# Regrouping the probability blocks on their way back from DRAM: one transfer per 32 destination partitions, or one per quarter of every partition's row

## The reference

```python
q = (query @ wq).reshape(bs, sq, HQ, DK).transpose(0, 2, 1, 3)
k = (key @ wk).reshape(bs, sk, HKV, DK)
v = (value @ wv).reshape(bs, sk, HKV, DV)
...
scores = jnp.einsum('bhqd,bhkd->bhqk', q, k) / scale
attn = jax.nn.softmax(scores + m[:, None, :, :], axis=-1)
out = jnp.einsum('bhqk,bhkd->bhqd', attn, v)
out = out.transpose(0, 2, 1, 3).reshape(bs, sq, HQ * DV)
return out @ wo
```

## Time and profile before

| | us |
|---|---|
| median of 3 runs | 1771.52 (1771.15 to 1772.29) |
| the profiled execution | 1774.46 |
| its span, first to last instruction | 1772.7 |
| TensorE busy | 1736.4 |
| VectorE busy | 1101.1 |
| GpSimd busy | 782.3 |
| ScalarE busy | 733.5 |

### The profile page before, as it was taken

One profiled execution on the slowest core, in us unless ns is written; L12 is line 12 of the kernel. 1 busy time (PEld: TensorE's weight loads), 2 busy tenths in 40 slices (PEclk: granted clock), 3 DMA queues, 4 the chain that ended last, 5 costly groups with the idle time before them and its releaser, 6 DMA issues.

```text
span 1772.7 us, 26431 instructions
## 1 busy us (share of the span) xinstructions
PE 1736.4 (98%) x8904; PEld 1579.1 (89%) x8904; DVE 1101.1 (62%) x2116; ACT 733.5 (41%) x1532; POOL 782.3 (44%) x588
## 2 busy tenths in 40 slices
PE   6999999999999999999999999999999999999998
PEld 6999999999888888888999999889999899999986
DVE  7631276566433333336666668898888888888845
ACT  5211210012333232222101014477887888888724
POOL 3223522125422222201222234487787877877634
PEclk9999999999999999999999999999999999999999
DMA  4212442235643333423433335699999999999833
GB/s 140 63 49 83 133 133 84 85 104 162 208 128 119 111 116 118 128 82 95 129 109 91 106 113 163 200 291 272 274 277 274 270 275 281 276 272 281 257 117 111
DMA packets 186403, 291.55 MB, mean 164 GB/s; under 512 B 48337, under 2 KB 146897, under 8 KB 185281
## 3 DMA queue, kind: packets, MB, share of 16 engines
q1 hardware_dynamic: 186304, 290.33, 55.7%
HBM read 193.01 MB, written 97.26 MB: 164 GB/s over the span
## 4 chain that ended last, share of the span: by engine, by line
PE 70%; DMA 8%; DVE 5%; POOL 2%; issue 2%; ACT 2%; SPq 1%; DVEq 0%; ACTq 0%; POOLq 0%
PE bank L200 65%; DMA probabilities<-q_rotated_then_x_rows 3%; DMA e_raw_wo<-in_wo 3%; SPq L1761 1%; DVE e_scores L1696 1%; POOL shared_operand_low L324 1%; PE bank L106 1%; DVE q_rotated_then_x_rows L1739 1%; PE bank L2317 1%; DVE e_p_t_low L1982 1%; PE bank L186 1%; PE bank L2330 1%; DMA aw_weights_then_ctx_rows<-in_wv 1%; DMA aw_weights_then_ctx_rows<-in_wk 0%; DMA ctx_raw<-in_ctx_t 0%
## 5 line engine op out<-in xcount | busy, mean ns | idle before, releaser
L200 PE MATMUL bank<-shared_operand_high,w_first_high 128*128 128x448 f32 (+1 forms) x768 | 279.1, 363 | 1.9 <-DVE shared_operand_low L558 1.2
L200 PE MATMUL bank<-shared_operand_high,w_first_low 128*128 128x448 f32 (+1 forms) x768 | 278.4, 362 | 0.0
L200 PE MATMUL bank<-shared_operand_low,w_first_high 128*128 128x448 f32 (+1 forms) x768 | 278.3, 362 | 0.0
L324 POOL TENSOR_TENSOR shared_operand_low<-ctx_raw,shared_operand_high 128x768 fp32r<-128x768 f32 x64 | 119.2, 1875 | 199.6 <-ACT shared_operand_high L320 199.4
L1704 ACT ACTIVATE e_scores<-e_scores,e_least 128x375 f32<-128x375 f32 x256 | 153.5, 601 | 44.9 <-DVE e_least L1696 44.9
L1452 POOL TENSOR_TENSOR w_first_low<-aw_weights_then_ctx_rows,w_first_high 128x1024 fp32r<-128x1024 f32 x30 | 72.2, 2407 | 221.1 <-ACT w_first_high L1420 221.1
L200 PEld LDWEIGHTS bank<-shared_operand_high,w_first_high 128*128 128x128 f32 x768 | 144.7, 188 | 13.1 <-POOL w_first_low L496 1.4
L200 PEld LDWEIGHTS bank<-shared_operand_low,w_first_high 128*128 128x128 f32 x768 | 144.8, 189 | 11.0
L200 PEld LDWEIGHTS bank<-shared_operand_high,w_first_low 128*128 128x128 f32 x768 | 144.6, 188 | 11.0
L320 ACT ACTIVATE shared_operand_high<-ctx_raw 128x768 fp32r<-128x768 f32 x64 | 52.8, 843 | 211.8 <-DMA ctx_raw<-in_ctx_t 193.2
L1696 DVE CUSTOM_DVE_ANT_0 e_scores<-bank,e_mask_then_layer_ffn 128x375 f32<-128x375 f32 x256 | 134.8, 529 | 0.0
(11 more groups left out here) (259 smaller groups left out, 4614.7 us busy)
## 6 DMA issues: line engine op xcount, KB each, us to landing
probabilities<-q_rotated_then_x_rows SPq DMA_DIRECT2D x64, 768.0 KB, 4.7
ctx_raw<-in_ctx_t SPq DMA_DIRECT2D x64, 384.0 KB, 3.9
e_shuffled_then_xn_t<-probabilities SPq DMA_DIRECT2D x128, 192.0 KB, 3.9
e_shuffled<-probabilities SPq DMA_DIRECT2D x128, 192.0 KB, 3.9
e_raw_wo<-in_wo SPq DMA_DIRECT2D x64, 256.0 KB, 4.8
aw_weights_then_ctx_rows<-in_wq SPq DMA_DIRECT2D x30, 512.0 KB, 4.0
q_rotated<-q_rotated_then_x_rows SPq DMA_DIRECT2D x64, 224.0 KB, 2.3
e_raw_then_a<-q_rotated SPq DMA_DIRECT2D x64, 224.0 KB, 5.0
```

Of the source, the lines that this page charges most:

```text
L200: mm = pe.matmul(out, stationary[a], moving[b], start=(first and i == 0), stop=(last and i == 2))
L324: pool.tensor_tensor(k.ctx_ring[1][slot][:, 2 * j:2 * j + 2, :], k.c_raw[:, j % 2], f32(k.ctx_ring[0][slot][:, 2 * j:2 * j + 2, :]), ALU.s ...
```

## The change

The same 768 KB move from `probabilities` to `pt_raw`, still in four transfers of 192 KB, in pieces of 384 values (1536 bytes) on both sides. They are grouped the other way round. Before, transfer j filled the 32 partitions of key block j with all four query blocks: the destination is 32 partitions by 4 by 384, the source is walked as (a: 32 rows, i: 4, 384). After, transfer i fills column block i of all 128 partitions: the destination is 128 partitions by 384, the source is walked as (j: 4, a: 32, 384). The waits, the semaphore and its count of 64, and the place in SyncE's order are the same.

```diff
-        for j in range(BLOCKS):
-            sp.dma_start(self.pt_raw[t][BLOCK * j:BLOCK * (j + 1)],
-                         self.k.p_dram[t, :, j].rearrange("(i a) x -> a i x", i=BLOCKS)).then_inc(
-                self.shuffled[t], 16)
+        for i in range(BLOCKS):
+            sp.dma_start(self.pt_raw[t][:, i], self.k.p_dram[t, BLOCK * i:BLOCK * (i + 1)].rearrange(
+                "a j x -> j a x")).then_inc(self.shuffled[t], 16)
```

## The result

The changed kernel takes 2143.54 us (median of 4 runs, 2137.36 to 2144.99) where the kernel before takes 1771.9 us beside it. The ratio is 1.2088, with a 95% interval of 1.2061 to 1.2114. The prediction was 2136, its range 1975 to 2400.

What follows compares the result with a forecast made beforehand. TensorE was taken to set the pace, DMA engines following with almost no slack. 357 us over 61 steps, plus 12, less 5, gave +364 on 1774.5: 2138.5, or 2136 as median; range 1975 to 2400.

Steps and rivals of the forecast that it cites:

- The mechanism: Block reads in attention steps: source outermost count 4 puts each transfer on the same 4 of 16 DMA engines; forecast 0.74.
- The first effect: Block transfers back: 128 partitions instead of 32 could go at 423 GB/s instead of 231, 1.5 us less DMA work per step.
- The step: One attention step on a loaded engine: 9.6 + 3.9 + 1.3 = 14.8 us instead of 8.95, bounds 12.6 and 18.8.
- The blocks' term: Blocks on a loaded engine, each step: 196,600 bytes at the middle rate of 20.4 GB/s, 9.6 us.
- the other bytes and the gap: Rest of a loaded engine's step: 104,200 bytes at 26.4 GB/s, 3.9 us, plus 1.3 us unfilled before blocks are read.
- the lower bound of 7.4: Least time in us for a loaded engine's blocks in a step, at 26.4 GB/s taken from the write out's 423.
- The estimate of 6.8 us: Blocks' share of a step at the page's about 27 GiB/s for an engine, somewhat below the prediction's lower bound.
- Rival 3: Block reads: four engines also stand in each other's way, staying at 14.4 GB/s; 2370 us; chance 0.13.
- The intervals: 61 step intervals, `carry_out` of step 2 to that of step 63, each 5.85 us longer: 357 us.
- 12 us on steps 0 and 1: Blocks of steps 0 and 1, in the queries' stage with weight tiles queued behind: 6 us added on each.
- 5 us of slack: Head start from blocks issued two steps ahead: 4 to 5 us, spent once in the first step, subtracted from the total.
- The granted clock: TensorE in the attention steps: cost of a lower clock from idling put at nothing; at 1.2 GHz its part would be 17.5 us.

Runs made afterwards that it cites:

- the two kernels with wide sources: Changed kernel with narrow writes regrouping: reads kept as four transfers with 128 source rows outermost, 1789.19 us; or one wide read, 1792.39 us.
- the kernel with two engines: Changed kernel with each quarter transfer cut into two of 64 partitions, source outermost count 2: 2621.89 us, ratio 1.482 against the kernel before.

## Why the prediction was right, point by point

**The mechanism.** Four engines instead of sixteen: shown, by the five updates of each transfer's semaphore where there were sixteen, and by the runs: going back to sixteen with the same destinations takes 354 of the 372 us away, and halving and doubling the bytes on a loaded engine moves the step with them. That the transfers share the same four is shown by the write's landings: twelve parts early, four late. Which of the sixteen they are, no run shows. By the Trainium skill ("DMA: Bandwidth & Descriptors", "Why a DMA increments its semaphore by 16 and not by 1") the count is the largest number up to 16 that divides both outermost counts; the runs with outermost counts of 128, 4 and 2 on the DRAM side, with 16, 4 and 2 engines by their semaphores, agree.

**The first effect,** wider destinations being faster, was real: 305 and 326 GB/s for wide reads in the two kernels with wide sources, against 230 for narrow ones. It is less than the 423 that I had taken from the write out: in the write's window there are no packets of the size of keys and values, which I had put "in the mix" of it "or behind it"; they come behind it. It has packets of 6144 bytes, and of 2048 from a `wo` tile. In the change the first effect is buried. On its own it was never isolated, since each kernel that had it paid for it with narrow writes.

**The step: 14.8 forecast, 14.64 measured.** The blocks' term was 9.6 us, the other bytes and the gap 3.9 + 1.3 = 5.2 us. From the first block packet to the last it is 10.25, and the rest is 4.5. So each part was within 16%, one too low and one too high, and the two errors cancel (the two measured parts are of steps 6 to 61, 14.76 us on average). The blocks' term was right by luck: the middle of two rates was a choice for want of a row, and neither end was the pace. Alone the four engines need 8.0 us, more than the lower bound of 7.4, which came from packets of 6144 bytes; what brings the time up to 10.25 is the slow start and the slower pace while all sixteen engines are busy, and neither was in the prediction. The estimate of 6.8 us was too low as well. Rival 3 had the four in each other's way at 14.4 GB/s for an engine; 196,600 bytes in 10.25 us are 19.2. The rest is shorter because the gap is: queries, keys and V keep the four busy until 1.0 us after the block issue, and the first block packet starts 0.3 us later, where I had 1.3. The sentence that the four engines go from one step's work to the next without another gap was right, and so was the place of `carry_out`, which is issued at least 7.1 us before it is needed.

**The intervals** were 61 times 14.64 - 8.95 = 5.69 us, 347 us, where 357 was forecast. The profiled spans differ by 2141.5 - 1772.7 = 368.8, where the sum had 364. `carry_out` of step 2 comes 5.1 us later (1140.58 against 1135.48), where I had put 12 us on steps 0 and 1. What follows `carry_out` of step 63 grew from 91.5 to 107.6 us (to the ends of the two spans), where I had written that it is unchanged and taken 5 us of slack off the whole. That term failed: the last write lands 5.8 us later after its issue (10.6 us to the blocks' issue, where it was 4.8), the `wo` behind the last blocks comes late as well, and nothing covers them at the end. 10 us too many in the steps, 7 too many at the start and 21 too few at the end: that the total is within 5 us is luck again.

**The granted clock.** I put it at nothing, on the ground that idling had not lowered it. That ground was wrong: the clock of the stage fell from 1.00 to 0.84. It still cost the steps nothing, for a reason that I had not given: in each of them the write out waits at least 7.1 us in the queue of the four engines. In the step shown TensorE ends its work at 1531.0 us and waits for the blocks until 1533.7. After `carry_out` of step 63 nothing covers it, the clock there is 0.88 (0.98 before) and TensorE is busy for 86.9 us instead of 81.6; up to 5 of the 16 us can be the clock's, which no run isolates.

**The signs.** 167 GB/s (165 said), TensorE's share 0.71 (0.6, as I left the lower clock out), its waits at the split of the blocks, landings of the blocks 4.8 to 10.5 us after their issues (5 to 12): as said. The DMA share of 0.54 lies above the 0.4 to 0.5 that I gave.

## What to carry to other kernels

When a transfer is regrouped, look at the outermost count on both sides, not only at the number of partitions and the piece: here a 4 on the DRAM side undid 128 partitions on the other and cost 21%, with bytes, pieces and issue count unchanged. A mean DMA share of 0.54 can hide engines that are full: look for a floor at k/16 in the slices (0.25 here for four engines), and for transfers of unchanged shape that all land late. A chain of waits that passes through a landing does not show that the landing is needed so early: count the time by which the next transfer is issued before its engines come to it, 7.1 us or more here. And where a load stands in a queue behind a long wait, another engine's queue can be worth more than a faster transfer: 7.5 to 10 us on the kernel before, for a few lines.

## What the runs showed of the hardware that I had not expected

TensorE's clock falls within a step and comes back. Windows of the changed kernel: a stretch in which TensorE issues nothing (1515.0 to 1519.2 us), and the first product after it.

```profile
1515.50:1516.20 0.70, 0.00 (x0) 0.00 (x0) 0.70 (x2) 0.70 (x2) 0.70 (x1) 1.00 0.24 84
1516.20:1517.20 1.00, 0.00 (x0) 0.00 (x0) 1.00 (x4) 1.00 (x3) 0.13 (x1) 1.00 0.25 92
1517.20:1518.50 1.30, 0.00 (x0) 0.00 (x0) 1.30 (x4) 1.30 (x5) 1.08 (x1) 0.97 0.17 44
1518.50:1519.50 1.00, 0.31 (x1) 0.34 (x2) 1.00 (x4) 1.00 (x4) 1.00 (x2) 0.50 0.28 98
```

The clock goes to 0.50, which is 1.2 GHz, while TensorE still stands, and it is 0.50 in the window of 1521.5 to 1524.5 us above too, with TensorE busy throughout: matmuls of 448 columns then start 0.37 us apart, and 0.20 at 1.00 two windows later. It comes back at about 1525.2 us. Not every stop does it: the next one, 1531.0 to 1533.7 us, is followed by matmuls 0.2 us apart, the full pace. In the kernel with two engines, whose stops are longer, the stage's clock is 0.73.
